# Splitting expert weights one attention group ahead, with four units in front of the first keys

## What is computed

```
x = x + _L0_attn_ref(_layernorm(x))                     # q = k = v = the normalised input
x = x + _L0_xattn_ref(_layernorm(x), ctx, mask, Wq, Wk, Wv, Wo, q_norm_w, k_norm_w)
x = x + _L0_ffn_ref(_layernorm(x), gate_w, bias, Wg, Wu, Wd, Sg, Su, Sd)

# cross-attention: q, k are RMS-normalised per head of 128
probs = softmax(q @ k.T / sqrt(128) + mask);  out = (probs @ v) @ Wo.T
# experts: top 4 of 16 by sigmoid score + bias
g = x @ Wg[e].T; u = x @ Wu[e].T; out += weight * (silu(g) * u) @ Wd[e].T
```

## Time and profile before

| | |
|---|---|
| median of 3 runs | 891.34 us (890.59 to 893.41) |
| the profiled execution | 896.45 us, its span 894.7 us |
| mean granted clock of PE | 0.968 |
| PE busy | 832.0 us (93%) |
| DVE / ACT / POOL busy | 544.3 / 510.5 / 522.2 us (61 / 57 / 58%) |
| moved by DMA | 142.47 MB |

### The profile page before, as it was taken

One profiled execution on the slowest core, in us unless ns is written; L12 is line 12 of the kernel. 1 busy time (PEld: TensorE's weight loads), 2 busy tenths in 40 slices (PEclk: granted clock), 3 DMA queues, 4 the chain that ended last, 5 costly groups with the idle time before them and its releaser, 6 DMA issues.

```text
span 894.7 us, 19354 instructions
## 1 busy us (share of the span) xinstructions
PE 832.0 (93%) x6773; PEld 452.6 (51%) x6773; DVE 544.3 (61%) x1030; ACT 510.5 (57%) x1012; POOL 522.2 (58%) x444
## 2 busy tenths in 40 slices
PE   6689699999999999999999999589779999999997
PEld 2664445644645545545545546245335555555553
DVE  5897676676577577577667667597942222222236
ACT  3678777577586586585685684354204444334431
POOL 6843567877867868859859859512223444444431
PEclk9699889999999999999999999799979999999999
DMA  8036606505515524434435415804044575778943
GB/s 310 3 81 197 217 1 210 188 21 201 182 51 183 165 85 160 154 116 141 141 117 155 128 48 169 331 20 166 1 139 168 188 258 188 256 262 290 388 150 141
DMA packets 51739, 142.47 MB, mean 159 GB/s; under 512 B 6368, under 2 KB 8416, under 8 KB 47328
## 3 DMA queue, kind: packets, MB, share of 16 engines
q1 hardware_dynamic: 43568, 116.93, 38.6%
q0 software_dynamic: 7520, 24.65, 7.9%
q10 hardware_dynamic: 592, 0.08, 0.1%
HBM read 97.85 MB, written 41.68 MB: 156 GB/s over the span
## 4 chain that ended last, share of the span: by engine, by line
PE 65%; DVE 13%; POOL 11%; issue 6%; ACT 2%; DMA 2%; SPq 0%; POOLq 0%; DVEq 0%
PE ps L1565 32%; POOL reg_h L625 5%; PE ps L1988 5%; PE ps L1990 5%; PE ps L1989 5%; POOL reg_h L621 4%; PE ps L1753 2%; PE ps L1967 2%; PE ps L2011 2%; PE ps L2013 2%; PE ps L2012 2%; POOL ring_mem L570 2%; PE ps L1740 2%; PE ps L1720 1%; PE ps L2035 1%
## 5 line engine op out<-in xcount | busy, mean ns | idle before, releaser
L1565 PE MATMUL ps<-wo_hi,reg_b 128*128 128x512 f16 x448 | 144.7, 384 | 8.9 <-DVE ring_mem L1181 8.9
L625 POOL TENSOR_TENSOR reg_h<-reg_h 128x512 f16<-128x512 f32 x88 | 110.0, 1260 | 37.4 <-ACT reg_h L846 32.8
L652 POOL DMA_INDIRECT y_rows<-reg_h,to_row x47 | 48.1, 1024 | 113.1 <-ACT reg_h L1020 113.1
L1565 PE MATMUL ps<-hT_hi,wq_hi 128*128 128x512 f16 x256 | 98.2, 383 | 16.5 <-DVE ring_mem L1172 16.5
L584 POOL TENSOR_TENSOR ring_mem<-kv,ring_mem 128x512 f16<-128x512 f32 x64 | 82.1, 1286 | 53.5 <-ACT ring_mem L780 53.5
L621 POOL TENSOR_SCALAR reg_h<-reg_h 128x512 f32<-128x512 f32 x56 | 92.1, 1644 | 27.9 <-ACT reg_h L844 27.9
L1565 PE MATMUL ps<-hT_lo,wq_hi 128*128 128x512 f16 x256 | 98.0, 383 | 0.0
L1565 PE MATMUL ps<-hT_hi,wq_lo 128*128 128x512 f16 x256 | 98.0, 383 | 0.0
L1565 PE MATMUL ps<-wo_lo,reg_b 128*128 128x512 f16 x224 | 85.9, 384 | 0.0
L1565 PEld LDWEIGHTS ps<-wo_hi,reg_b 128*128 128x128 f16 x448 | 44.1, 98 | 65.5 <-issue 11.0
L1988 PE MATMUL ps<-ring_mem,reg_h 128*128 x188 | 71.9, 383 | 4.4 <-DVE reg_h L1515 4.3
(11 more groups left out here) (323 smaller groups left out, 2040.4 us busy)
## 6 DMA issues: line engine op xcount, KB each, us to landing
w_split<-reg_h SPq DMA_DIRECT2D x96, 256.0 KB, 2.3
ring_mem<-w_split SPq DMA_DIRECT2D x16, 1536.0 KB
reg_h<-in_wgu SPq DMA_DIRECT2D x64, 256.0 KB, 3.5
stage<-in_wq SPq DMA_DIRECT2D x8, 1024.0 KB, 6.6
stage<-in_wo SPq DMA_DIRECT2D x8, 1024.0 KB, 4.8
reg_h<-in_wd SPq DMA_DIRECT2D x32, 256.0 KB, 3.1
wkv_st<-in_wkv SPq DMA_DIRECT2D x8, 512.0 KB, 7.3
ring_mem<-in_x_half SPq DMA_DIRECT2D x8, 256.0 KB, 6.7
```

The lines of the kernel that those rows point to most:

```text
L625: pool.tensor_tensor(hl[:, 1, :], st, hl[:, 0, :], ALU.subtract).then_inc(pre_split, 1)
L652: pool.indirect_dma_start(y_rows, bass.IndirectOffsetOnAxis(ap=to_row[:, r - 1:r], axis=0), y[r % 2], None).then_inc(scattered[r % 2], 16)
L1565: last = pe.matmul(dst, lhsT(c), rhs(c), start=(m == 0), stop=(m == n - 1))
```

## The change

The unit numbers turn by four. Units 0 to 3 of group i + 1 are now done at the front of stage i (with ACT's copy and scaling), units 4 to 11 in its t-loop and behind it, so a group is complete one stage before its attention. The last stage has no units. Group 0 must be complete at the end of the first stage. For this its units 0 to 3 are loaded at the very start, in place of the first output weights, into four further places (`first_mem`: the second half of `stage`, and `wo_hi` and `wo_lo`, which are empty then). ACT copies these four and then scales these four in front of the first keys, and POOL subtracts in front of `k_square_lo`. Units 4 to 7 are loaded into the same places, each after the store in that place has landed, and units 8 to 11 into `reg_h`; ACT takes them behind `q_parts(0, 0)` to `q_parts(0, 7)`, DVE makes their low halves. The first output weights are loaded when the stores of units 4 to 7 have landed.

```diff
+        first_mem = [stage[:, 2048:3072], stage[:, 3072:4096],
+                     *(w[:, :, :].rearrange("p h d -> p (h d)").bitcast(F32) for w in (wo_hi, wo_lo))]
+        first_st = [w[:, 0:512] for w in first_mem]
+        first_hl = [w[:, 512:1024].bitcast(F16).rearrange("p (z n) -> p z n", z=2) for w in first_mem]
...
# SP
-            sp.dma_start(wo_st, wo[0]).then_inc(wo_in, 16)
+            for q in range(SLOTS):
+                sp.dma_start(first_st[q], wgu[0, :, q, :]).then_inc(pre_in[q], 16)
...
+            def first_store(q):
+                if q < SLOTS:
+                    sp.wait_ge(pre_split, q + 1)
+                else:
+                    sp.wait_ge(pre_split_dve, q + 1 - SLOTS)
+                hl = (first_hl if q < 2 * SLOTS else pre_hl)[q % SLOTS]
+                sp.dma_start(w_split[q // ITEMS, :, 2 * BANK * (q % ITEMS):2 * BANK * (q % ITEMS + 1)],
+                             hl.rearrange("p z n -> p (z n)")).then_inc(pre_stored[q % SLOTS], 16)
...
             query_weights(1)
+            for q in range(SLOTS):
+                first_store(q)
+                sp.wait_ge(pre_stored[q], 16)
+                c = q + SLOTS
+                src = wgu[c // ITEMS, :, c % ITEMS, :] if c % ITEMS < KC else wd[c // ITEMS, :, c % ITEMS - KC, :]
+                sp.dma_start(first_st[q], src).then_inc(pre_in[q], 16)
             sp.wait_ge(hT_ps, NT)
             for q in range(SLOTS):
-                pre_load(0, q)
-            pre_early(0, first=True)
+                sp.wait_ge(pre_in[q], 32)
+                pre_load(0, 2 * SLOTS + q)
+            for q in range(SLOTS, 2 * SLOTS):
+                first_store(q)
+            for q in range(SLOTS):
+                sp.wait_ge(pre_stored[q], 32)
+            sp.dma_start(wo_st, wo[0]).then_inc(wo_in, 16)
+            for q in range(2 * SLOTS, UNITS):
+                first_store(q)
+                pre_load(1, q - 2 * SLOTS)
             with sp.Fori(1, G - 1) as g:
-                pre_late(g - 1)
+                pre_units(g, range(SLOTS))
                 output_weights(g)
                 query_weights(g + 1)
-                pre_early(g)
-            pre_late(G - 2)
+                pre_units(g, range(SLOTS, UNITS))
+            pre_units(G - 1, range(SLOTS))
             output_weights(G - 1)
-            pre_early(G - 1)
-            pre_late(G - 1, more=False)
+            pre_units(G - 1, range(SLOTS, UNITS), more=False)
...
# POOL, iteration(i, att, proj)
-                if att:
-                    for q in range(2 * SLOTS, UNITS):
-                        pre_lo(i, q)
+                if att and proj:
+                    for q in range(SLOTS):
+                        pre_lo(i + 1, q)
...
                 if proj and att:
-                    for q in range(2 * SLOTS):
+                    for q in range(SLOTS, UNITS):
                         pre_lo(i + 1, q)
...
+            def first_lo(q):
+                pool.wait_ge(pre_scaled_act, q + 1)
+                pool.tensor_tensor(first_hl[q][:, 1, :], first_st[q], first_hl[q][:, 0, :],
+                                   ALU.subtract).then_inc(pre_split, 1)
+
+            for q in range(SLOTS):
+                first_lo(q)
             k_square_lo(0, 0)
...
# ACT
+            def first_hi(q):
+
+                us, n = q % SLOTS, q // SLOTS
+                act.wait_ge(pre_in[us], 16 * n + 16)
+                if n:
+                    act.wait_ge(pre_stored[us], 16 * n)
+                st, hl = (first_st, first_hl) if n < 2 else (pre_st, pre_hl)
+                act.activation(hl[us][:, 0, :], st[us], ACT.Copy, scale=WS).then_inc(pre_hi, 1)
...
-                if att:
-                    for q in range(2 * SLOTS, UNITS):
-                        pre_unit_hi(i, q)
+                if att and proj:
+                    for q in range(SLOTS):
+                        pre_unit_hi(p, q)
...
-                    if not att and k >= 2:
-                        pre_unit_hi(0, k - 2)
+                    if not att:
+                        first_hi(SLOTS + k)
...
-                        pre_unit_hi(p, t)
+                        pre_unit_hi(p, SLOTS + t)
...
-                if not att:
-                    for q in (6, 7):
-                        pre_unit_hi(0, q)
...
+            for q in range(SLOTS):
+                first_hi(q)
+            for q in range(SLOTS):
+                act.activation(first_st[q], first_st[q], ACT.Copy, scale=WS).then_inc(pre_scaled_act, 1)
             k_parts(0, 0)
             k_parts(0, 1)
...
# DVE, first stage
-                    if not att and k >= 2:
-                        pre_lo(k - 2)
+                    if not att:
+                        pre_lo(SLOTS + k)
...
-                if not att:
-                    for q in (6, 7):
-                        pre_lo(q)
```

More of the change, by code:

```diff
@@ L386, in pre_load, with pre_store @@
                 sp.dma_start(pre_st[q % SLOTS], src.rearrange("o p n -> p (o n)")).then_inc(pre_in[q % SLOTS], 16)
[L388 to L392, removed]
+            def pre_store(g, q):
+                sp.wait_ge(pre_split, UNITS * g + q + 1 - 2 * SLOTS)
                 dst = w_split[bass.ds(2 * g + q // ITEMS, 1), :, 2 * BANK * (q % ITEMS):2 * BANK * (q % ITEMS + 1)]
@@ L405, in output_weights, with pre_units @@
                 sp.dma_start(wo_st, wo[g]).then_inc(wo_in, 16)
-            def pre_early(g, first=False):
-                for q in range(2 * SLOTS):
-                    pre_store(g, q, first)
-                    pre_load(g, q + SLOTS)
-            def pre_late(g, more=True):
-                for q in range(2 * SLOTS, UNITS):
+            def pre_units(g, units, more=True):
+                for q in units:
                     pre_store(g, q)
-                    if more:
-                        pre_load(g + 1, q - 2 * SLOTS)
+                    if q + SLOTS < UNITS:
+                        pre_load(g, q + SLOTS)
+                    elif more:
+                        pre_load(g + 1, q + SLOTS - UNITS)
             query_weights(1)
+            for q in range(SLOTS):
[4 more added lines that the diff above has]
+                sp.dma_start(first_st[q], src).then_inc(pre_in[q], 16)
             sp.wait_ge(hT_ps, NT)
             for q in range(SLOTS):
-                pre_load(0, q)
-            pre_early(0, first=True)
+                sp.wait_ge(pre_in[q], 32)
[8 more added lines that the diff above has]
+                pre_load(1, q - 2 * SLOTS)
             with sp.Fori(1, G - 1) as g:
-                pre_late(g - 1)
+                pre_units(g, range(SLOTS))
                 output_weights(g)
                 query_weights(g + 1)
-                pre_early(g)
-            pre_late(G - 2)
+                pre_units(g, range(SLOTS, UNITS))
+            pre_units(G - 1, range(SLOTS))
             output_weights(G - 1)
-            pre_early(G - 1)
-            pre_late(G - 1, more=False)
+            pre_units(G - 1, range(SLOTS, UNITS), more=False)
             sp.wait_ge(ssq_q_ps, G)
@@ L1244, in pre_lo @@
                 dve.wait_ge(pre_hi, q + 1)
-                hl = pre_hl[q % SLOTS]
-                dve.scalar_tensor_tensor(hl[:, 1, :], pre_st[q % SLOTS], WS, hl[:, 0, :],
+                st, hl = (w[q % SLOTS] for w in ((first_st, first_hl) if q < 2 * SLOTS else (pre_st, pre_hl)))
+                dve.scalar_tensor_tensor(hl[:, 1, :], st, WS, hl[:, 0, :],
                                          ALU.mult, ALU.subtract).then_inc(pre_split_dve, 1)
```

8 lines of the change are left out of this document (4 added, 4 removed).

## The result

The changed kernel takes 888.64 us in the median (886.86 to 892.38, 18 runs), the kernel before 892.12 us (889.96 to 900.88, 18 runs, which take in the three shown above). The ratio is 0.9951 with a 95% interval of 0.9934 to 0.9968: 4.4 us faster, between 2.9 and 5.9. (The medians themselves lie 3.5 us apart.) I had forecast 8.4 us, 882.9, with a range to 888.0. The direction was right, the size about twice too large.

The account below looks back on a forecast made before the run. PE's waits at the first boundary (7.8 us) and in the last stage (8.9 us) led, with DVE the bound behind the latter. Terms -8.7 and +0.3 gave -8.4 us: 888.05 profiled, 882.9 as median, range 877.5 to 888.

Parts of the forecast that it names:

- The last stage: Attention stage 7: without its four front units, masks begin 7.2 us earlier and PE's matmuls keep the clock; -8.7 us.
- Loop stages: Stages in the loop: still four units in front and eight behind, only their numbers turn; 0.
- In front of the keys: First stage: added ACT copies and POOL subtractions stay hidden; overlap with DVE's row normalisation 0 to 0.9 us, taken 0.
- The chain on SP: First stage: four store-and-load round trips at 2.75 us a step delay projection 4; the stage gets 4.0 us longer.
- the boundary: End of the first stage: 4 us of saved loads offset the 4.0 us longer stage; PE resumes at 111.5 against 111.25; +0.3.
- rival D: First stage: SP's round trips at dense prices, step 4.45 and load 4.0, give 891 us; no change 0.06, slower 0.03.
- rival B: First stage: the clock falls after PE idles 2.5 and 1.6 us before projections 3 and 4; 886 us, chance 0.2.
- The base: Whole kernel: the profiled 896.45 us is 5.1 us above the median 891.34, a difference carried over unchanged.
- The chances: Whole kernel: faster 0.88, same 0.08, slower 0.04; a change under 2.7 us counts as the same.

Follow-up runs that it names:

- e5: The changed kernel, with POOL waiting for the second variance ahead of the two key squares; 889.56 us, ratio 0.9961 to the kernel before.
- e9: The changed kernel without ACT's wait for the stores of units 4 to 7 before copying units 8 to 11; 886.99 us, ratio 0.9945.
- e8: The kernel before, with POOL's last addition and four context subtractions in the first self-attention gated on DVE's probability multiplications; 890.49 us, ratio 0.9972.
- e1: The kernel before, unchanged, measured once more; 892.34 us, ratio 1.0015.
- e10: The changed kernel, with SP also waiting for each load of units 4 to 7 before storing the next unit; 896.88 us, ratio 1.0054.
- e7: The changed kernel without the waits removed in e3 and e9, plus the POOL wait of e5 and the gate of e8; 883.7 us, ratio 0.9887.
- e3: The changed kernel, with SP loading units 4 to 7 without waiting for the stores of units 0 to 3 to land; 884.15 us, ratio 0.9894.

## Why the prediction missed

**The last stage** (-8.7 us). Right in mechanism and nearly in size. Masks 7.2 us earlier: 63.65 - 56.41 = 7.2. PE's wait 1.7: 1.6. DVE the bound behind it: the shift reached the end of the stage. The clock held in the stage, as assumed. About 8 us of 8.7 arrived.

**Loop stages** (0). Right: from the masks of stage 1 to those of stage 6 it is 326.66 us in before and 326.68 in after.

**In front of the keys** (0). Wrong in a part, without a price. The four copies, four scalings and two key steps fitted as counted: ACT was done at 60.57, ahead of the variance. I looked for POOL's collision at DVE's row normalisation; it came at the two small instructions before, 1.8 us against my 0 to 0.9. It cost nothing in time only because the transfers were later still (e5).

**The chain on SP** (+4.0 in the stage, +0.3 at the boundary). This is the step that failed. From the mark, PE's eighth projection was taken at 98.64 - 55.04 = 43.6 us against 91.27 - 56.20 = 35.1: 8.5 us longer, not 4.0, and +4.8 at the boundary, not +0.3. The terms one by one:
- The store of unit 0 landed 74.45 - 55.04 = 19.4 us behind the mark, forecast 19.2.
- A step took 3.67 us (74.47 to 78.10 to 81.77 to 85.47), not 2.75. I took the store's 2.0 us from a row in which the store was alone and the load came behind it. In this chain the order is the other way round: the store stands behind a load just issued. Three steps: 2.8 us. The kernel before had such a store too, and I used its price only for rival D (the store issued at 100.51, right behind the load of 100.03; transfers, kernel before):

```profile
w_split<-reg_h SPq DMA_DIRECT2D x1, 256.0 KB, 3.8
```

- Unit 8 has a wait that I read over: `pre_stored[us]` at 32, so its copy needs the landed store of unit 4, though it lies in other memory. I had followed only its load. 1.6 us (e9). That store is late by SP's order, not by its data: DVE had the low half of unit 4 at 78.83 (row below), but SP first waited for load 7, issued the loads of units 8 to 11 and came to the store at 89.03.

```profile
78.14 0.69 DVE L1284 SCALAR_TENSOR_TENSOR stage<-stage 128x512 f16<-128x512 f32 x1 [3.09 <-ACT stage L883]
```

- The clock fell behind the waits of 1.18 and 2.10 us (rival B, which thought of 2.5 and 1.6). The nine matmuls from 85.24 to 88.87 took 3.63 us; at the 0.216 us a piece of those around them it would be 1.9, so about 1.7 us of PE's time. Nothing in the trace carries it to the end of the stage: behind it ACT waits for load 7 (1.58) and for the store of unit 4 (1.42) and for no result of PE, and PE itself stands again for 1.41 us:

```profile
95.84 0.39 PE L1600 MATMUL ps<-hT_hi,wq_hi 128*128 128x512 f16 x1 [1.41 <-DVE ring_mem L1210]
```

So rival B's event came and its price didn't. The steps and unit 8, 2.8 and 1.6, make 4.4 of the 4.5 us that the forecast lacked.

What the boundary gives back, the loads of units 6 to 11 that before stood in front of stage 0, was right: 8.5 - 3.7 = 4.8, as 4.0 - 3.7 = 0.3.

With a step of 3.67 and a load of 3.2 my own formula for rival D gives 75.35 + 3 x 3.67 + 3.2 + 2.9 - 86.0 = 6.5 us of shift, and 1.6 for unit 8 makes 8.1. The same formula gives 3.6 for the forecast's prices and 9.6 for D's dense ones, so D was the right picture at half its way. (Its bound has a slip: with P = 5 and its load of 4.0, 3P + L is 19; it takes a load of 5 to reach 20.) The section of the Trainium skill that the prediction cites, DMA: Bandwidth & Descriptors, "Anatomy of one DMA", is on transfers that GpSimd issues, and these are SP's. Neither its estimate of 2.6 us nor the lone store's 2.0 was the price in this order; the trace has 3.24 to 3.31. The sum with measured terms, -8 + 4.8 = -3.2 us, is inside the measured 2.9 to 5.9.

**The base.** I carried the difference of 5.1 us between the profiled execution and the median over unchanged. The profiled time of before was indeed long, and the difference of the two profiles (7.1 us) looks like a confirmation of the forecast where the medians say 3.5. Against e8, the same kernel but for the gate, its span was 6.1 us longer: 2.8 ahead of the mark, 1.0 in stage 0, where the lower clock lasted until 9 us behind the first masks and not 7, 1.7 behind the last aggregate of the last stage, the rest in between. e1 shows that the part ahead of the mark can reach 9. The 1.7 I haven't traced.

**The chances.** 0.88 for faster was borne out, though the interval, from 2.9 us, only just clears the 2.7 that I had set as the limit. The range to 888.0 missed by 0.6 us. I had put 0.06 on the chain at dense prices and nothing between it and the forecast, though the forecast's store had its price from a row in another order; the middle belonged in the range.

## What to carry to other kernels

When a transfer must land before the next is issued, take the price of the one that stands behind another, in the new order, and then multiply by the steps. List every semaphore that a moved instruction waits for, also those that guard other memory: they are free until their transfer is late. Before two profiles are subtracted, set a mark after the part that no edit touched, and measure stages from it.

## What the runs showed of the hardware

A 256 KB store to device memory landed in 2.05 us when nothing was queued ahead, in 3.24 to 3.31 us right behind a load of the same size, and in 5.3 us behind four (e10).

A DVE instruction with two SBUF inputs can be held up by POOL working from SBUF for much longer than one POOL instruction. The first 128x512 multiplication, 0.69 us at its shortest, took 0.88, 2.50, 3.44, 11.77 and 12.42 us in five profiles, and between 0.69 and 3.19 in the five others without the gate; with the gate it took 0.69 (e8) and 1.25 (e7). Instructions of 16 elements took 1.05 and 1.08 us while POOL subtracted, and 0.17 and 0.18 with POOL held off (e5). The Trainium skill, SBUF — State Buffer, section "SBUF: two separate sides", says that the port pair shared by the two is an exclusive lock, held for the whole instruction, and counts a DVE instruction with two SBUF inputs among those that need it against a POOL instruction that reads SBUF. The traces agree that DVE stands while POOL works; that it may stand over several POOL instructions in a row is the runs' addition: 11.77 us in e1 and 12.42 in e3, each ending 0.5 to 0.6 us after POOL's last one, and 4.54 us in stage 0 of e9.

The granted clock fell to the lower level at about 85.3 us, after waits of 1.18 and 2.10 us within 5 us, and was back by 89. The single wait of 1.61 us in the last stage left it at the upper one, 1.00 from 562 to 566. Length alone doesn't decide: behind the wait of 3.15 us at the first boundary of the changed kernel the clock fell, at about 116; in e9 it stayed at 1.00 through waits of 2.86 and 2.80 us at the same place, and had fallen earlier, behind 0.82 and 2.03 us. What the clock goes by isn't shown here.
